# Bias sums of eight head pairs in sixteen rows of one PSUM bank, and their stores one row at a time

## The reference, cut to what matters

```python
x = x + xattn(ctx, layernorm(x), f, f, ln1_w, ln1_b, ln2_w, ln2_b, Wq, Wkv, Wout)   # x: (16, 1024, 512), ctx: (16, 64, 512)
x = x + tanh(layernorm(x) @ weight @ aux_weight1 @ aux_weight2 + ffn_bias)

def xattn(ctx, lat, shift, scale, ...):            # 16 heads of 64, 64 context rows per batch
    k, v = split((layernorm(ctx) * ln1_w + ln1_b) @ Wkv)
    q = (layernorm(lat) * ln2_w + ln2_b) @ Wq
    q = q * (1 + scale) + shift                    # one number per batch and head, f = (16, 16)
    attn = softmax(q @ k.T / 8)
    return (attn @ v) @ Wout
```

## Time and profile before

| | us |
|---|---|
| median of 3 timed runs | 2051.66 (2050.03 to 2053.55) |
| the profiled execution, its own time | 2051.34 |
| its span, first to last instruction | 2049.5 |
| PE busy | 2027.4 (99%) |
| PE weight loads busy | 1681.4 (82%) |
| DVE, POOL, ACT busy | 1520.5 (74%), 1349.7 (66%), 1319.4 (64%) |
| mean busy share of the DMA engines 196-211, 211-226, 226-241, 241-256 us | 0.89, 0.96, 1.01, 0.93 |

### The profile page before, as it was taken

The page is one execution under the profiler, slowest core; times in us unless marked ns, Lnnn a source line. Parts: engine busy times, 40 slices in busy tenths (PEclk is TensorE's granted clock), DMA queues, the critical chain, the costliest instruction groups (busy, mean ns, idle before and its releaser), DMA issues.

```text
span 2049.5 us, 31380 instructions
## 1 busy us (share of the span) xinstructions
PE 2027.4 (99%) x9180; PEld 1681.4 (82%) x9180; DVE 1520.5 (74%) x2414; ACT 1319.4 (64%) x3005; POOL 1349.7 (66%) x1466
## 2 busy tenths in 40 slices
PE   9999999999999999999999999999999999999998
PEld 7777878888888888888888888888888888888887
DVE  7567777776777777777777777777777777787776
ACT  4455667666766666666666667666666666666654
POOL 3136766766676776767676776767677676767564
PEclk9999999999999999999999999999999999999999
DMA  7657988878787887878788787878767576666653
GB/s 263 197 176 211 271 232 245 251 225 248 222 227 206 219 223 208 226 204 231 195 232 219 208 224 206 230 197 217 211 185 211 174 207 179 200 184 191 178 170 118
DMA packets 502490, 431.54 MB, mean 211 GB/s; under 512 B 54832, under 2 KB 408240, under 8 KB 502320
## 3 DMA queue, kind: packets, MB, share of 16 engines
q1 hardware_dynamic: 502320, 429.54, 74.6%
HBM read 251.33 MB, written 178.06 MB: 210 GB/s over the span
## 4 chain that ended last, share of the span: by engine, by line
PE 86%; DVE 3%; DMA 2%; ACT 2%; issue 2%; POOL 2%; SPq 2%; DVEq 0%; ACTq 0%; POOLq 0%
PE bank L161 34%; PE bank L1176 21%; PE bank L166 17%; PE bank L1179 10%; DMA m_scratch<-evac 1%; PE bank L880 1%; PE bank L879 1%; POOL area L1458 1%; POOL area L1465 1%; DVE N_lo L987 0%; DVE area L1319 0%; SPq L321 0%; DVE row_max L1324 0%; DVE turned L1341 0%; ACT bank L992 0%
## 5 line engine op out<-in xcount | busy, mean ns | idle before, releaser
L1458 POOL TENSOR_TENSOR area<-area,row_max 128x256 f32<-128x256 f32 x512 | 353.8, 712 | 145.8 <-DVE row_max L1324 145.8
L1176 PE MATMUL bank<-N_hi,pT_hi 128*128 128x512 f32 x1024 | 398.7, 389 | 2.6 <-DVE N_lo L987 1.3
L161 PE MATMUL bank<-M_hi,xT_hi 128*128 128x512 f32 x1024 | 398.7, 389 | 0.0
L161 PE MATMUL bank<-M_lo,xT_hi 128*128 128x512 f32 x1024 | 398.7, 389 | 0.0
L1176 PE MATMUL bank<-N_lo,pT_hi 128*128 128x512 f32 x1024 | 398.6, 389 | 0.0
L1227 ACT CAST pT_hi<-turned 128x512 fp32r<-128x512 f32 x256 | 159.1, 622 | 337.4 <-DVE turned L1341 337.4
L1465 POOL TENSOR_TENSOR area<-area,row_inv 128x512 f32<-128x512 f32 x256 | 269.2, 1052 | 114.7 <-DVE row_inv L1333 114.6
L1482 POOL TENSOR_TENSOR area<-area 128x512 f32<-128x512 f32 x127 | 165.4, 1303 | 239.3 <-ACT area L1266 239.3
L1330 DVE TENSOR_REDUCE row_sum<-area 128x8 f32<-128x512 f32 x256 | 174.4, 681 | 167.5 <-ACT area L1222 166.7
L1350 DVE TENSOR_TENSOR pT_lo<-turned,pT_hi 128x512 fp32r<-128x512 f32 x256 | 196.1, 766 | 119.2 <-ACT pT_hi L1227 119.2
L166 PE MATMUL bank<-M_hi,xT_lo 128*128 128x512 f32 x1024 | 273.9, 389 | 0.8 <-POOL xT_lo L1025 0.7
(11 more groups left out here) (183 smaller groups left out, 3923.3 us busy)
## 6 DMA issues: line engine op xcount, KB each, us to landing
p_scratch<-area SPq DMA_DIRECT2D x256, 256.0 KB, 2.6
p_moved<-p_scratch SPq DMA_DIRECT2D x512, 128.0 KB, 4.3
area<-x_dram SPq DMA_DIRECT2D x128, 256.0 KB, 4.5
area<-x_turned_dram SPq DMA_DIRECT2D x128, 256.0 KB, 4.0
x_scratch<-area SPq DMA_DIRECT2D x127, 256.0 KB, 3.0
x_moved<-x_scratch SPq DMA_DIRECT2D x508, 64.0 KB, 3.5
y_dram<-area SPq DMA_DIRECT2D x127, 256.0 KB, 3.6
land<-m_scratch SPq DMA_DIRECT2D x120, 256.0 KB, 2.8
```

The source lines that it names most:

```text
L161: mm = eng.matmul(ps, sh, mv, start=(n == 0), stop=False)
L1176: pe.matmul(O_ps[:], st(pT_hi, k), n_cols(mv, k), start=(k == 0 and mv is N_hi), stop=False)
L1458: last = pool.tensor_tensor(s, s, row.to_broadcast([P, 2, 4, J2]), ALU.subtract)
```

## The change

`bdv` holds one column of ones for each head instead of a block of ones. A shifted view of it (`to_row`) as stationary operand puts the two sums of a pair into rows `row` and `row + 4` of the output and zeros elsewhere, and the eight pairs of a half accumulate into one bank. So each half has one bank, one copy of 16 rows by ACT (at kv step 28 and at M product 12) and one buffer. The 16 rows of a half are stored in 16 DMAs of one row: four each in kv steps 28 to 31 for half 0, four each at the end of slots 0 to 3 for half 1. PE's first two score products wait for the two copies. `load_x(6)`, in slot 4, waits for all stores of half 1, whose buffer it overwrites.

```diff
         k0_raw = stage[2]
-        ku, bias_out = ctx_in[0:2], (ln2_b_row, ln1_b_row, ln2_w_row)
-        head_ones = bdv[:, 0:P]
+        ku, bias_out = ctx_in[0:2], (ln1_b_row, ln2_b_row)
+        ONE_AT = (DH - 2, DH + 2)
         ku_hi, ku_lo = (x2T_hi, x2T_lo), (xT_hi, xT_lo)
...
         s_ku, s_kuh, s_kul, s_kb, s_kbo = (sem(n) for n in ("s_ku", "s_kuh", "s_kul", "s_kb", "s_kbo"))
-        s_kbst = [sem(f"s_kbst{i}") for i in range(3)]
+        s_kbst = [sem(f"s_kbst{i}") for i in range(2)]
         s_kvst = [sem(f"s_kvst{i}") for i in range(2)]
...
                 sp.dma_start(ctx_in[i % 3], ctx_t[i]).then_inc(s_ctx[i % 3], 16)
-
-            def store_bias(k):
-                half, p = k // 8, k % 8
-                sp.wait_ge(s_kbo, k + 1)
-                for h in range(2):
-                    rows = bias_scratch[half * 8:half * 8 + 8].rearrange(
-                        "b (q h s k j) -> q k h b s j", q=2, h=2, s=2, k=4)[p // 4, p % 4, h:h + 1]
-                    sp.dma_start(rows, bias_out[k % 3][h * DH:h * DH + 1, :].rearrange("o (b s j) -> o b s j", b=8, s=2)).then_inc(s_kbst[k % 3], 16)
 
...
                                  kv_out[i % 2].rearrange("p (b j) -> p b j", b=8)).then_inc(s_kvst[i % 2], 16)
-                if step == "kv" and i >= 20:
-                    store_bias(i - 20)
+                if step == "kv" and i >= 28:
+                    store_bias(sp, 0, i - 28)
                 if step == "wst":
...
                     load_wst(sp, 1)
-            store_bias(12)
             for q in s_kvst:
...
                 sp.dma_start(m_scratch[1, dc, g // 2], m1_raw[k]).then_inc(s_m1w, 16)
-                if k in (2, 4):
-                    store_bias(12 + k // 2)
             sp.wait_ge(s_m, 16)
             load_wst(sp, 3)
-            store_bias(15)
 
...
 
-        def bias_evacuate(act, k):
-            act.wait_ge(s_kb, k + 1)
-            at_least(act, s_kbst[k % 3], 32 * (k // 3))
-            act.copy(bias_out[k % 3], kb_ps[k % 2][:]).then_inc(s_kbo, 1)
+        def bias_evacuate(act, half):
+            act.wait_ge(s_kb, PAIRS * (half + 1))
+            act.copy(bias_out[half][0:H, :], kb_ps[half][0:H, :]).then_inc(s_kbo, 1)
 
...
                 if step == "kv" and i >= 16:
-                    if i >= 20:
-                        bias_evacuate(act, i - 20)
+                    if i == 28:
+                        bias_evacuate(act, 0)
                     if i < 30:
...
             for half in range(2):
-                own = slice(half * DH, (half + 1) * DH)
-                dve.memset(bdv[own, own].bitcast(F32), 1.0).then_inc(s_ones, 1)
+                dve.memset(bdv[half * DH:(half + 1) * DH, ONE_AT[half]:ONE_AT[half] + 1].bitcast(F32), 1.0).then_inc(s_ones, 1)
             for step, i in dve_front + later_steps:
...
             pe.wait_ge(s_kul, k + 1)
-            at_least(pe, s_kbo, k - 1)
-            pe.matmul(kb_ps[k % 2][:], head_ones, ku_hi[k % 2][:], start=True, stop=False)
-            pe.matmul(kb_ps[k % 2][:], head_ones, ku_lo[k % 2][:], start=False, stop=True).then_inc(s_kb, 1)
+            half, p = k // PAIRS, k % PAIRS
+            row = p // 4 * 8 + p % 4
+            to_row = bdv[:, ONE_AT[0] - row:ONE_AT[0] - row + P]
+            pe.matmul(kb_ps[half][:], to_row, ku_hi[k % 2][:], start=(p == 0), stop=False)
+            pe.matmul(kb_ps[half][:], to_row, ku_lo[k % 2][:], start=False, stop=(p == PAIRS - 1)).then_inc(s_kb, 1)
 
...
             at_least(sp, s_xout[r], 16 * (u // RING))
+            if u == 6:
+                sp.wait_ge(s_kbst[1], 16 * H)
             if u in (2, 3):
...
 
+        def store_bias(sp, half, four):
+            q, h = four // 2, four % 2
+            if four == 0:
+                sp.wait_ge(s_kbo, half + 1)
+            rows = bias_scratch[half * 8:half * 8 + 8].rearrange("b (q h s k j) -> q h k b s j", q=2, h=2, s=2, k=4)[q, h]
+            own = bias_out[half][four * 4:four * 4 + 4, :].rearrange("k (b s j) -> k b s j", b=8, s=2)
+            for k in range(4):
+                sp.dma_start(rows[k:k + 1], own[k:k + 1]).then_inc(s_kbst[half], 16)
+
         def load_bias(sp, b):
             if b < 2:
-                for i, w in enumerate(s_kbst):
-                    sp.wait_ge(w, 32 * len(range(i, PAIRS if b == 0 else 2 * PAIRS, 3)))
+                sp.wait_ge(s_kbst[b], 16 * H)
             sp.dma_start(bias, bias_scratch[bass.ds(b, 1), :].to_broadcast([P, INNER])).then_inc(s_bin, 16)
...
                     ku_split_hi(act, 14 + c // 2)
-                if c in (2, 4, 7, 12):
-                    bias_evacuate(act, {2: 12, 4: 13, 7: 14, 12: 15}[c])
+                if c == 12:
+                    bias_evacuate(act, 1)
                 if c == 11:
...
             store("C")
+            if t < 4:
+                store_bias(sp, 1, t)
             if t < 2:
...
                         pe.wait_ge(s_ml, 8 * q + 8)
-                        pe.wait_ge(s_kbo, 15 + q)
+                        pe.wait_ge(s_kbo, 1 + q)
                     elif m == 0:
```

## The result

| | us |
|---|---|
| changed kernel, median of 6 runs | 2060.49 (2059.77 to 2062.19) |
| before, 6 runs beside it | 2050.91 (2050.03 to 2053.55) |
| ratio | 1.0047, 95% interval 1.0034 to 1.0059 |
| span of the profiled execution, after and before | 2058.8 and 2049.5 |

The change costs 9.6 us, 0.47%. Forecast were 2057.6 and "slower"; the range of 2049 to 2061.5 holds the result.

What follows compares the result with a forecast made beforehand. PE was taken as the bound, busy 99%, with SP's DMA queue full beside it. Terms 0.2 + 1.5 + 5.3 + 2.0 - 2.7 = +6.3 us on 2051.3 gave 2057.6 us; range 2049 to 2061.5 with 8 in 10.

Steps and rivals of the forecast that it cites:

- PE in the M step: M products before slot 0: PE's waits of 1.1 and 2.5 us go, first score product 3.6 us sooner, at 145.8.
- the wait for bdv: Before the first fold of N: a new PE wait of 2 to 4 us for DVE's bdv, as a sign.
- V and m1: Setup's end: later load_bias and V use up PE's lead, m1 landing unchanged; net +0.2 us, bounds -2.7 and +2.0.
- Slots 0 and 1: Bias stores at these slots' ends partly fit SP's room; land(1) arrives late, +1.5 us, bounds 0 and 1.9.
- Slots 2 and 3: SP is full here, so both groups of four bias stores count in full: 2 x 2.64 = +5.3 us.
- PE would wait some 3 us before a tile product in each of slots 5 and 6: Slots 5 and 6: sign that SP's lateness reaches PE, as waits of some 3 us each before a tile product.
- Wait in load_x(6): Slot 4: SP stands still until the last bias store lands, +2.0 us, bounds 1.2 and 2.9.
- Given back: SP's queue up to 260 us: its 2.7 us of waits are swallowed by lateness, -2.7 us, bounds 0 and 2.7.
- Sum: Whole kernel: the terms add to +6.3 us, giving 2057.6 us; bounds +1.1 and +12.1.
- free stores: Rival, SP in slots 2 and 3: bytes pace SP, 5.3 us shrink to about 0.5; 2052.8 us, chance 0.27.
- surviving gain: Rival: M step's gain survives, chain from 155.81 starts 2.7 to 3.6 us sooner; 2046.4 to 2048.6 us, chance 0.11.
- The double wait: Rival, load_x(6) in slot 4: store queues 4 to 5 us instead of 2; +10, 2061.5 us, chance 0.10.

Runs made afterwards that it cites:

- e5: Changed kernel with only half 0's bias stores (kv steps 28 to 31) made as four-row stores: 2055.41 us, ratio 1.0020 to the kernel before.
- e2: Changed kernel with half 1's 16 one-row stores moved to setup's end, early slot 0 and ends of slots 0 and 1: 2054.80 us, ratio 1.0022 to before.
- e6: Changed kernel with only half 1's bias stores (slots 0 to 3) made as four-row stores: 2054.83 us, ratio 1.0017 to the kernel before.
- e8: Changed kernel with half 1's four store groups cut in four shapes, to read SP's issue times; one execution took 2061.1 us.
- e11: Changed kernel with the eight one-row stores of slots 2 and 3 made twice, second time into an unread scratch tensor: 2065.22 us, ratio 1.0074 to before.
- e10: Changed kernel with 16 unused 128x512 matmuls in PE's idle time ahead of the first fold: 2060.36 us, ratio 1.0050 to the kernel before.
- e7: Changed kernel with four-row stores, half 1's in SP's two gaps, V of batch 0 early, three m1 stores ahead of it: 2048.21 us, ratio 0.9978 to before.
- e3: Changed kernel with V of batch 0 loaded ahead of the last four bias stores: 2060.59 us, ratio 1.0045 to the kernel before.

## Why the prediction was right, and where not

- **PE in the M step**: scores forecast for 145.8, found at 145.63. Right; likewise load_bias (145.1, found 145.49), V's issue (145.9, found 146.32), and the wait for bdv (2 to 4 us, found 4.3).
- **V and m1, +0.2 us**: the term that was mis-sized most. PE's first tile product is 2.45 us late, and e5 puts 5.1 us of the total on half 0's stores. I had let the four bias issues that no longer stand among the m1 stores pay for the later start (last m1 issue near 149.7, score read unchanged). The eight m1 issues then took 5.7 us, 0.6 and 0.8 each, where they had taken 0.39 to 0.51 between bias stores, and the read moved with the first of them, from 154.92 to 157.96. The profiled execution was already 2.2 us late at kv step 20 (its store at 106.65 against 104.48), ahead of any change in the K steps; other kernels with the same setup had 104.5 to 106.2 there, so that is a difference between executions, and the effect of half 0 is taken from e5's timed runs. In e2, e6, e8 and e11, whose half 0 is the same, PE's first tile product is 1.3 to 2.6 us late. That e5 gives more than this is the lead that the change could have had: the first p_scratch store stands at 158.97 in e5, at 161.09 before and at 163.64 after.
- **Slots 0 and 1, +1.5 us through land(1)**: the size was nearer than the path. Slot 2's first p_scratch store came 5.1 us late, 2.65 more than PE at the tile product. The instruction that carried it is not land(1): the group at 166.74 stands ahead of p_moved(0), issued at 170.59 in place of 167.25, and PE waits 2.6 us for pT_hi behind it, in place of 1.3. That makes PE 3.8 us late at 177.00, and the granted clock of 0.50 behind this wait adds 1.5 us, as told above. A low clock was not in my forecast at all; e10 shows no cost of it at the end. I had looked for what stands directly behind the stores and stopped at the first load.
- **Slots 2 and 3, +5.3 us**: right. SP lost 2.7 us in slot 2 (5.1 to 7.8 at xT(4)) and 2.2 in slot 3 (10.0 at xT(5)); e2 gives back 5.7 for two groups. That PE would wait some 3 us before a tile product in each of slots 5 and 6 did not come so: it is idle for 4.1 us from 200 to 260 us, and no wait there is over 1.3.
- **Wait in load_x(6), +2.0 us**: wrong. The weight load ahead of x(6) ends at 210.60 and x(6) starts at 210.73: 0.13 us. The store started at 209.0 and was down 1.7 us after, as the chain after shows for one of half 0: I had priced the landing by the 4.49 us of the earlier trace rows, which was met at a share of the DMA engines of 0.60 (209 GB/s, so 0.9 MB over the 4.49 us), and by k_raw; at this store the share was 0.02.

```profile
143.72 1.69 DMA bias_scratch<-area
```

- **Given back, -2.7 us**: too much. SP's queue still waits 3.7 us from 184 to 260 us, against 2.7 before; the largest two:

```profile
SPq L1065 <- POOL area L1465: 1.9, 1, 1.9
SPq L820 <- PE bank L875: 1.1, 3, 0.4
```

   By the shift of SP (10.0 at xT(5), 9.5 at V of batch 1) some 0.5 us came back.
- **Sum**: the rows of the two profiled executions give 2.45 + 2.65 + 4.9 + 0.1 - 0.5 = 9.6. This follows SP's lateness through one pair of executions, whose spans differ by 9.3, so it must come out near the loss and is no proof of the parts; e5 and e6 put about half of the loss on each half's stores. Against these rows the term of slots 2 and 3 was right. The false +2.0 half cancelled the 3.4 us missing at the start and in slots 0 and 1, and the -2.7 was 2.2 too much. So the direction rests on a mechanism that the runs confirm, SP's issue time in full slots, and that the number came within 3 us is in part luck.
- **The rivals**: free stores fell by e2 and e11, where SP's queue time reached the end. The Trainium skill's "DMA: Bandwidth & Descriptors", section "Anatomy of one DMA — SWDGE (gpsimd) path", gives about 50 ns for the sequencer's dispatch and about 2.0 us fixed for a DMA, both for the GpSimd path. The 50 ns are not what SP's queue shows, with medians of 346 to 627 ns here. The 2.0 us are nearer to the 1.69 us of the quiet store than my 4.49 was. Of the surviving gain 0.22% is seen in e7, with its other edits; that it comes from the M step's wait isn't isolated. The double wait did not occur.
- **What was not seen**: that the shape of the store, and not the number of stores, could be the cheap thing to change. The rows to compare stood in the trace: a 128x512 DMA issues in 0.32 to 0.43 us and the one-row store in 0.64.

## What to carry to other kernels

On a queue that is full, count issue time, and read it from rows of the same shape at both ends: one small store may issue slower than a large one, and the same row into another layout may issue faster (e11). Look for the idle stretches of the same queue before putting small transfers at the end of a step. When a wait is removed, follow the next two waits behind it (here V, then the m1 stores); removing the first of them alone (e3) moves nothing, and a landing time should be taken from a row with the same traffic beside it.

## What the runs showed of the hardware

- SP's issue time differs by the store's shape, and not by its bytes. One row of `bias_scratch` took 600 ns with 8 pieces of 128 bytes and 624 to 627 with 16 (medians), four rows with 32 pieces 346 (263 to 530), one row into one stretch of 2 KB 403 to 422. Two rows with 16 pieces took 669, 602, 322 and 279 ns, so the shape alone doesn't fix it.
- From the start of its issue the 2 KB store landed in 4.49 us at a share of the DMA engines of 0.60, and in 1.69 us at 0.02.
- ACT's copy of 16 rows of 512 took 574 ns (median of two), of 128 rows 582, and of 128 rows of 256 numbers 380 (L761): here the time goes by the row's length, not by the rows.
- The granted clock fell to 0.50 behind idle times of PE of 4.1 us in e2, 4.0 in e6 and 2.6 in the changed kernel, and stayed full in e10 behind one of 3.3. In the changed kernel e10 shows no cost of it at the end.
